# Routing steps of the expert passes in other slots, and the residual sum on GpSimd

## What is computed

```python
x = x + 0.5 * _L0_ffn_ref(_layernorm(x, axis=-1), ...)   # ffn0a
x = x + _L0_attn_ref(_layernorm(x, axis=-1), ...)
x = x + 0.5 * _L0_ffn_ref(_layernorm(x, axis=-1), ...)   # ffn0b
x = x + 0.5 * _L1_ffn_ref(_layernorm(x, axis=-1), ...)   # ffn1a
x = x + _L1_attn_ref(_layernorm(x, axis=-1), ...)
x = x + 0.5 * _L1_ffn_ref(_layernorm(x, axis=-1), ...)   # ffn1b
```

## Time and profile before

| | |
|---|---|
| median of three runs | 2052.0 us |
| profiled execution, its span | 2051.49 us, 2049.7 us |
| PE busy | 1723.2 us (84%) |
| VectorE, ScalarE, GpSimd busy | 1351.5, 1004.0, 736.8 us (66%, 49%, 36%) |
| granted PE clock, mean | 0.924 |

### The profile page before, as it was taken

How to read it: one execution, slowest core, us unless ns; L and a number is a source line. 1 busy time by engine, 2 the same in 40 slices (tenths; PEclk the granted TensorE clock), 3 DMA queues, 4 the chain that set the end, 5 groups by cost and what they waited for, 6 DMA issues and landing times. The chain is left out here.

```text
span 2049.7 us, 26334 instructions
## 1 busy us (share of the span) xinstructions
PE 1723.2 (84%) x8440; PEld 1206.2 (59%) x8440; DVE 1351.5 (66%) x4086; ACT 1004.0 (49%) x1687; POOL 736.8 (36%) x693
## 2 busy tenths in 40 slices
PE   3888869899899899968888699989967775989998
PEld 2666645545555555436666477767755664767776
DVE  4676658778778778536656466666667765666665
ACT  3555415555555565644554355455532223555554
POOL 3444411311312211114544355555520102555555
PEclk9999959999999999979888899999988897999999
DMA  4222211111110110003232211211100001121111
GB/s 130 84 78 69 64 28 30 18 24 28 18 34 18 21 31 18 10 25 103 78 104 74 95 42 42 75 50 42 42 1 0 0 0 42 51 84 47 47 52 52
DMA packets 58086, 94.98 MB, mean 46 GB/s; under 512 B 9297, under 2 KB 16850, under 8 KB 57954
## 3 DMA queue, kind: packets, MB, share of 16 engines
q1 hardware_dynamic: 55842, 91.08, 15.9%
q10 hardware_dynamic: 2112, 2.30, 0.4%
HBM read 76.76 MB, written 2.88 MB: 39 GB/s over the span
## 5 line engine op out<-in xcount | busy, mean ns | idle before, releaser
L909 ACT ACTIVATE att_probs<-banks 128x1024 f32<-128x1024 f32 (+3 forms) x384 | 306.1, 812 | 194.1 <-PE banks L820 192.0
L401 ACT ACTIVATE banks<-banks 128x512 f32<-128x512 f32 x384 | 223.3, 582 | 246.3 <-PE banks L319 239.9
L1034 DVE CUSTOM_DVE_ANT_0 banks<-banks,att_mask 128x128 f32<-128x128 f32 (+3 forms) x512 | 234.4, 525 | 70.6 <-PE banks L801 70.1
L801 PE MATMUL banks<-arena 128*128 128x512 f32 (+3 forms) x768 | 249.1, 406 | 27.9 <-DMA arena<-att_parts 15.3
L949 POOL TENSOR_SCALAR_AFFINE_SELECT att_probs<-att_probs 128x512 f32<-128x512 f32 x128 | 81.6, 637 | 419.7 <-ACT att_probs L909 419.7
L801 PEld LDWEIGHTS banks<-arena 128*128 128x128 f32 x768 | 132.7, 197 | 150.5 <-issue 90.8
L438 POOL TENSOR_TENSOR ffn1a_hid_l<-ffn1a_hid,ffn1a_hid_h 128x512 fp32r<-128x512 f32 x128 | 165.6, 1294 | 153.0 <-ACT ffn1a_hid_h L406 153.0
L438 POOL TENSOR_TENSOR ffn1b_hid_l<-ffn1b_hid,ffn1b_hid_h 128x512 fp32r<-128x512 f32 x128 | 165.3, 1292 | 152.1 <-ACT ffn1b_hid_h L406 152.1
L820 PE MATMUL banks<-arena 128*128 128x512 f32 (+3 forms) x768 | 204.4, 351 | 0.5 <-ACT att_probs L909 0.4
L1036 DVE TENSOR_REDUCE att_mx<-banks 128x1 f32<-128x512 f32 x256 | 162.2, 684 | 32.0 <-PE banks L801 31.8
L839 PE MATMUL banks<-att_probs,att_v_aug 128*32 128x512 f32 (+3 forms) x1536 | 166.4, 505 | 0.6 <-POOL att_probs L949 0.5
(11 more groups left out here) (390 smaller groups left out, 3890.8 us busy)
## 6 DMA issues: line engine op xcount, KB each, us to landing
ffn0a_share<-weight_rows SPq DMA_DIRECT2D x128, 128.0 KB, 3.0
ffn0b_share<-weight_rows SPq DMA_DIRECT2D x128, 128.0 KB, 3.0
ffn1a_share<-weight_rows SPq DMA_DIRECT2D x64, 256.0 KB, 4.3
ffn1b_share<-weight_rows SPq DMA_DIRECT2D x64, 256.0 KB, 4.5
arena<-att_parts SPq DMA_DIRECT2D x16, 384.0 KB
arena<-att_parts SPq DMA_DIRECT2D x128, 48.0 KB
w_raw<-in_ffn_w_dram SPq DMA_DIRECT2D x12, 256.0 KB, 3.2
out_dram<-x SPq DMA_DIRECT2D x8, 256.0 KB, 2.3
```

Of the source, the lines that this page charges most:

```text
L401: act.activation(gate if c < NSCALED else sil[:], gate, ACT.Silu).then_inc(silu_done, 1)
L801: mm = pe.matmul(bank[:, at:at + width], q_st[:, n % 3, t * P:(t + 1) * P], k_pad[:, n % 2, j, c * G:c * G + width], start=True, stop=True ...
L909: act.activation(probs[:, unit % NPROB, 2 * pair:2 * pair + 2, 0:c], score_ps[:, pair, :, 0:c], ACT.Exp, scale=SCALE).then_inc(exped, 1)
L1034: ins = dve.tensor_tensor_reduce(now, now, mask[:, G - width:G], 1.0, -3e38, ALU.add, ALU.max, best)
```

## The change

The table of slots is another one, and `norm` is cut in two steps of two tiles. In ffn0, `turn`, `xh` and `xl` become early steps: they are made for group h + 2 in the last slot, h's rows having been read. The routing is cut into r1 to r5 with the same instructions. The pieces go from slots 1 and NC // 2 to (3, 6) and (5, 10). The turned output is no longer read by VectorE: ScalarE copies it, halved, to SBUF (`take`), and GpSimd adds it to x (`add`). PE's waits on `misc` now ask for that copy (`y_read`).

```diff
--- before.py
+++ after.py
@@ -181,12 +181,14 @@
     ROUTE = 12 if first else 8
 
     if first:
-        slot = dict(stats=7, aggr=7, rstd=8, norm=8, turn=0, xh=0, xl=0, logit=2, lout=2, lturn=3,
-                    r1=3, r2=4, r3=5, r4=5, cturn=6, yout=2, yturn=4, y=4)
+        slot = dict(stats=0, aggr=1, rstd=1, norm=3, norm2=4, turn=8, xh=8, xl=8, logit=1, lout=1, lturn=2, r1=2, r2=2,
+                    r3=3, r4=4, r5=5, cturn=7, yout=2, yturn=5, y=6)
+        early = ("stats", "aggr", "rstd", "norm", "norm2", "turn", "xh", "xl")
     else:
-        slot = dict(stats=13, aggr=13, rstd=14, norm=14, turn=1, xh=1, xl=1, logit=3, lout=3, lturn=5,
-                    r1=5, r2=7, r3=9, r4=10, cturn=11, yout=2, yturn=7, y=8)
-    early = ("stats", "aggr", "rstd", "norm")
+        slot = dict(stats=11, aggr=12, rstd=12, norm=14, norm2=15, turn=1, xh=1, xl=1, logit=3, lout=3, lturn=4, r1=4,
+                    r2=5, r3=7, r4=8, r5=8, cturn=10, yout=2, yturn=6, y=7)
+        early = ("stats", "aggr", "rstd", "norm", "norm2")
+    PIECES = (3, 6) if first else (5, 10)
 
     def rows(g):
         return slice((g - g0) * G, (g - g0 + 1) * G)
@@ -206,8 +208,8 @@
                 f(g)
 
     def piece_at(g, c):
-        n = 2 * (g - g0 - 1) + (0 if c == 1 else 1)
-        return n if ahead is not None and g > g0 and c in (1, NC // 2) and n < ahead.count else None
+        n = 2 * (g - g0 - 1) + (0 if c == PIECES[0] else 1)
+        return n if ahead is not None and g > g0 and c in PIECES and n < ahead.count else None
 
     with ExitStack() as ctx:
         def sem(name):
...
@@ -242,7 +245,7 @@
         comb_turned, comb_t = sem("comb_turned"), sem("comb_t")
         rows_out = [sem(f"rows_out{q}") for q in range(2)]
         share_in = [sem(f"share_in{e}") for e in range(SLOTS)]
-        y_out, y_turned, y_added = sem("y_out"), sem("y_turned"), sem("y_added")
+        y_out, y_turned, y_read, y_added = sem("y_out"), sem("y_turned"), sem("y_read"), sem("y_added")
         gate_done, up_done, silu_done, scaled, hidden = (sem(s) for s in
             ("gate_done", "up_done", "silu_done", "scaled", "hidden"))
         high_cut, low_cut, down_done = sem("high_cut"), sem("low_cut"), sem("down_done")
@@ -307,6 +310,7 @@
 
             def cturn(g):
                 pe.wait_ge(route, (g + 1) * ROUTE)
+                at_least(pe, y_read, g - 1)
                 for t in range(TG):
                     mm = pe.transpose(misc[0:NE, t * P:(t + 1) * P], comb[:, t, :], k.ident)
                 mm.then_inc(comb_turned, 1)
@@ -343,7 +347,7 @@
                 elif g + 1 < end:
                     pe.wait_ge(comb_t, g + 2)
                 else:
-                    pe.wait_ge(y_added, g)
+                    pe.wait_ge(y_read, g)
                 for t in range(TG):
                     mm = pe.transpose(misc[:, t * P:(t + 1) * P], y_t[:, t * P:(t + 1) * P], k.ident)
                 mm.then_inc(y_turned, 1)
@@ -367,7 +371,12 @@
         def _(act):
             def norm(g):
                 act.wait_ge(rstd_done, 2 * g + 2)
-                for t in range(TG):
+                for t in range(TG // 2):
+                    act.activation(xn[:, t, :], k.x[:, tile_of(g, t)], ACT.Identity, bias=nshift[:, t:t + 1],
+                                   scale=rstd[:, t:t + 1])
+
+            def norm2(g):
+                for t in range(TG // 2, TG):
                     ins = act.activation(xn[:, t, :], k.x[:, tile_of(g, t)], ACT.Identity, bias=nshift[:, t:t + 1],
                                          scale=rstd[:, t:t + 1])
                 ins.then_inc(norm_done, 1)
@@ -410,19 +419,27 @@
                 at_least(act, y_turned, g)
                 act.activation(y_t[:], y_ps, ACT.Copy).then_inc(y_out, 1)
 
+            def take(g):
+                act.wait_ge(y_turned, g + 1)
+                at_least(act, y_added, g)
+                act.activation(y_tok[:], misc, ACT.Copy, scale=0.5).then_inc(y_read, 1)
+
             for h in range(g0 - 2, end):
                 for c in range(NC):
                     if h >= g0:
                         if slot["yout"] == c and h > g0:
                             yout(h - 1)
+                        if slot["y"] == c and h > g0:
+                            take(h - 1)
                         silu(h, c)
                         if h * NC + c > g0 * NC:
                             high(h * NC + c - 1)
                         if piece_at(h, c) is not None:
                             ahead.high(act, piece_at(h, c))
-                    chain(h, c, (("norm", norm), ("xh", xh), ("lout", lout), ("r1", r1), ("r2", r2), ("cturn", cturn)))
+                    chain(h, c, (("norm", norm), ("norm2", norm2), ("xh", xh), ("lout", lout), ("r1", r1), ("r2", r2), ("cturn", cturn)))
             high(end * NC - 1)
             yout(end - 1)
+            take(end - 1)
 
         @block.gpsimd
         def _(pool):
@@ -437,6 +454,10 @@
                 pool.wait_ge(high_cut, num + 1)
                 pool.tensor_tensor(hid_l[:, num % NH, :], hid[:, num % NH, :], hid_h[:, num % NH, :].bitcast(F32),
                                    ALU.subtract).then_inc(low_cut, 1)
+
+            def add(g):
+                pool.wait_ge(y_read, g + 1)
+                pool.tensor_tensor(k.x[:, rows(g)], k.x[:, rows(g)], y_tok[:], ALU.add).then_inc(y_added, 1)
 
             if ahead is not None:
                 ahead.clear(pool)
@@ -447,8 +468,11 @@
                             low(h * NC + c - 1)
                         if piece_at(h, c) is not None:
                             ahead.low(pool, piece_at(h, c))
+                        if slot["y"] == c and h > g0:
+                            add(h - 1)
                     chain(h, c, (("rstd", invert),))
             low(end * NC - 1)
+            add(end - 1)
 
         @block.vector
         def _(dve):
...
@@ -526,24 +559,15 @@
                     step(top(ext, top_sb), g)
                     step(dve.memset(top_sb[:, :, 4:8], PAD), g)
                 else:
-                    step(dve.memset(top_sb[:, :, 2:8], PAD), g)
-                pause(dve, k)
-                for t in range(TG):
-                    ins = dve.match_replace(mark[:, t, :], top_sb[:, t, :], ext[:, t, :], TAKEN)
-                step(ins, g)
-                if not first:
                     dve.wait_ge(tanh_done, g + 1)
                     step(dve.tensor_scalar(sig[:], th[:], 0.5, 0.5, ALU.mult, ALU.add), g)
 
-            def r4(g):
+            def r5(g):
+                if first:
+                    step(taken(ext, mark), g)
                 at_least(dve, comb_turned, g)
                 step(dve.scalar_tensor_tensor(comb[:], mark[:, :, 0:NE], TAKEN, sig[:], ALU.is_equal, ALU.mult), g)
                 assert count[0] == ROUTE, count[0]
-
-            def add(g):
-                dve.wait_ge(y_turned, g + 1)
-                dve.scalar_tensor_tensor(k.x[:, rows(g)], misc, 0.5, k.x[:, rows(g)], ALU.mult, ALU.add)\
-                   .then_inc(y_added, 1)
 
             def scale(g, c):
                 num, n = g * NC + c, g * NSCALED + c
@@ -568,14 +592,11 @@
             for h in range(g0 - 2, end):
                 for c in range(NC):
                     if h >= g0:
-                        if slot["y"] == c and h > g0:
-                            add(h - 1)
                         if c < NSCALED:
                             scale(h, c)
                         hide(h, c)
                     chain(h, c, (("stats", stats), ("aggr", aggr), ("xl", xl), ("r1", r1), ("r2", r2), ("r3", r3),
-                                 ("r4", r4)))
-            add(end - 1)
+                                 ("r4", r4), ("r5", r5)))
 
 
 def parcel(arena):
```

More of the change, by code:

```diff
@@ L232, in phase_moe @@
         hid_h, hid_l, y_t = sb("hid_h", [P, NH, G], F32R), sb("hid_l", [P, NH, G], F32R), sb("y_t", [P, G])
+        y_tok = sb("y_tok", [P, G])
         gate_ps, up_ps, y_ps, misc = k.banks[:, 0:3, :], k.banks[:, 3:6, :], k.banks[:, 6, :], k.banks[:, 7, :]
@@ L503, in r1, with taken @@
                     step(top(ext, top_sb), g)
+            def taken(rest, dst):
+                pause(dve, k)
+                for t in range(TG):
+                    ins = dve.match_replace(dst[:, t, :], top_sb[:, t, :], rest[:, t, :], TAKEN)
+                return ins
             def r2(g):
@@ L508, in r2 @@
                     step(dve.memset(top_sb[:, :, 2:8], PAD), g)
-                    pause(dve, k)
-                    for t in range(TG):
-                        ins = dve.match_replace(gmark[:, t, :], top_sb[:, t, :], gext[:, t, :], TAKEN)
-                    step(ins, g)
-                    step(dve.tensor_scalar(pen[:].rearrange("p (e t) -> p e t", t=TG),
-                                           gmark[:, :, 0:5].rearrange("p t e -> p e t"), TAKEN, OUT, ALU.not_equal,
-                                           ALU.mult), g)
                 else:
@@ L521, in r3, with r4 @@
             def r3(g):
```

(9 more changed lines are left out.)

## The result

Four runs of the changed kernel took 1934.5 to 1943.96, median 1936.8 us; four of the kernel before beside them had median 2063.2. The ratio is 0.9396, 95% interval [0.9315, 0.9478]: **faster by 6%**. The profiled execution took 1934.5 against 2051.49, 117.0 less where 84.8 was forecast; 1936.8 lies in the range given, 1.8 above its lower bound. The kernel before took 2030 to 2077 in all its runs, at a mean granted clock of 0.936 down to 0.908, so the clock of one stage in its trace belongs to that execution.

A forecast was written before the change was run, and what follows sets the result against it. PE bounds the expert passes, with holes in it. Gains of 20.9, 30.3, 21.2 and 16.8 over six groups per pass, minus 4.4 at the ends, make 84.8: 2051.5 to 1966.7, 1967 against the median, range 1935 to 1995.

The forecast's parts named there:

- the 2.96, 2.12 and 1.92: PE holes forecast to go: 2.96 in ffn1 at the normalizations, in ffn0 2.12 before turning rows, 1.92 before turning weights.
- The base of 37.1 in ffn1: ffn1's group period without its hole, before new delays are added: 40.23 - 2.96 - 0.16 = 37.1 us.
- that of 22.0 in ffn0: ffn0's group period without its three holes, before new delays are added: 27.24 down to 22.0 us.
- The inverse: ffn1, slot 12: GpSimd waits about 0.5 for VectorE, spends 1.3, and PE comes 1.0 late per group.
- The sum: Residual sum on GpSimd, 1.27 in a slot with 0.8 free: 0.5 on PE per group, bounds 0 and 1.3.
- The late broadcast: ffn0, weights turned in slot 7: VectorE waits 1.5 to 2.0 for their broadcast, 1.4 on PE per group.
- The 1.0 for the pieces: ffn0b: a weight piece of 1.30 shares slot 6 with the sum and slot 3 with norm, 1.0 more per group.
- The ends: Pass ends: later last sum costs 1.3 per pass, ffn1's last two groups 0.9; 4.4 lost in all.
- Everything new is covered: Rival, chance 0.12: PE's extra work hides all new delays; periods 22.1, 22.6, 37.2, 37.2, total 1925.
- The broadcast becomes the bound: Rival for ffn0, chance 0.18: hole at slots 2 and 3 reaches 2, the clock falls, adding 1.4; total 1994.
- The port: Rival, chance 0.04: added GpSimd work holds VectorE's routing steps, two per ffn0 group, one per ffn1 group; total 2010.
- the slower rival: Rival, chance 0.02: GpSimd's sum and inverse each idle PE over 2 per group, the clock falling after each; total 2093.

The follow-up runs named there:

- inverse3: The changed kernel with ffn1's statistics moved to slot 2 and aggregation and inverse to slot 3: 1931.1 us.
- cturn6: The changed kernel with the turning of ffn0's routing weights back in slot 6 instead of 7: 1923.7 us.
- sum8: The changed kernel with ffn1's residual sum in slot 8 instead of 7: 1940.6 us.
- sum_only: The kernel before with only the residual sum moved, ScalarE copying the turned output and GpSimd adding it: 2029.2 us, ratio 0.989.
- best: The changed kernel with the edits of cturn6 and inverse3 and the residual sum back on VectorE in its new slots: 1911.4 us.
- both: The changed kernel with the edits of cturn6 and inverse3, the sum staying on GpSimd: 1916.6 us.
- late_sum: The kernel before with ffn0's residual sum, still on VectorE, in slot 5 instead of 4: 2020.3 us, ratio 0.988.

## Why the prediction was right

**How near it was.** The range held by 1.8, and the gain was 117.0 in the trace for 84.8. The 32 too few are all on one side: 5.0 in ffn0a, 8.8 in ffn0b, 11.2 in the two of ffn1, 7.1 outside the periods. In ffn1 the measured 37.7 and 37.6 lie below even the 37.8 that the range allowed. So what follows is a right account of the holes with prices set too high. (The bounds of the groups add up to 1934 and 1990, not 1935 and 1995.)

**What bounds it, and the holes.** Right: the 2.96, 2.12 and 1.92 went with the steps named, the clock came up, and the holes behind the inverse and the broadcast stand where they were put. The one forecast two slots after the sum in ffn1 did not come. The base of 37.1 in ffn1 is 37.0 (`inverse3`), that of 22.0 in ffn0 is 21.9 (`cturn6`).

**The inverse, forecast 1.0, measured 0.59.** GpSimd waited 0.19, not 0.5, for VectorE, and its two instructions took 1.24. The next subtraction came 2.73 after the last, 0.6 beyond a slot.

**The sum, forecast 0.5 per group, measured 0 in ffn1.** This term was wrong, by 6 over the twelve periods of ffn1; in ffn0a too nothing of it shows (21.9 in `cturn6`, where 22.0 + 0.1 + 0.5 would be due). A slot was taken as 2.1; the one with the sum lasts 2.5, with or without the sum. In a plainer slot it costs 0.3 (`sum8`). ScalarE's copy was free in the changed kernel, as forecast: it starts at 1717.93 and the silu behind it is not late. It is not free in every slot: in `sum_only` it stood right behind the tanh, for which ScalarE had waited 1.65, the silu came late, and PE had a hole of 0.58 per group.

**The late broadcast, forecast 1.4, measured 1.28 in ffn0a**, with VectorE's wait 1.82 in the group shown and 1.8 to 2.7 over the six, forecast 1.5 to 2.0. In ffn0b it brought 0.58. The 1.0 for the pieces is right with the sum on GpSimd (22.9 in ffn0b against 21.9 in ffn0a in `cturn6`, with a hole of 1.05 behind the slot where piece and sum meet). With the sum on VectorE (`best`) both passes take 22.5 and that hole is gone, so the price is that of the two together. Added to the broadcast's it was too much, since the waits cover each other: 23.5, not 25.0. Those 8.8 are the largest miss of any one pass.

**The ends, forecast -4.4, measured +2.8 in all.** The cost of the later last sum is real: from the last turned logits of ffn1b to the end are 69.75 in `both` and 68.08 in `best`, 1.7 where 1.3 was forecast. What made up for it was not tested. The stretch with the first attention alone varies by 7 and more between traces, so 2.8 is no firm number.

**The rivals.** "Everything new is covered" gave 1925, 12 too fast: broadcast and inverse were not covered. "The broadcast becomes the bound" had the right mechanism, but its holes, 0.48 and 0.39 in the group shown and 1.35 at most, stayed below 2, and the clock stayed up. Its condition, that the clock falls from a hole of 2 on, holds only in some groups: the last three periods of ffn0a before have 2.11 to 2.15 at a clock of 1.00. The port did hold VectorE, 1.23 for an instruction that took 0.23 in `cturn6`, in the rows shown above; no loss beyond the two holes showed. Inside the six periods GpSimd's remainder never came more than 1.35 late for PE (in ffn0a, behind a broadcast 2.71 late; 1.15 in ffn1a, 1.08 in ffn0b), short of the 2 of the slower rival. The sum's move cost 5.5 (1936.8 against 1931.3), and 5.2 between `both` and `best`. The rule of the Trainium skill (GPSIMD Engine Reference, Engine selection), to keep such work on VectorE, is right in sign by these totals, though not in ffn0a alone (130.97 with the sum on GpSimd, 135.23 without); its 19 was too much, since most of the doubled time lies beside other work.

## What to carry to other kernels

Before moving work to another engine, move it by one slot: here the wait for an operand made in the same slot cost more than the engine's time (one number, 1.2%, against 5.5 us lost by the other engine). Price an addition by the length of the slot it falls in, not by the mean slot, and do not add the prices of two delays that stand close together. When a step is placed later, look for what reads its product through the slowest path (here DRAM), and place that step as early as its input is ready.

## What the runs showed of the hardware

The granted clock did not follow the holes alone. In ffn0b of the kernel before, holes of 0.75, 1.92 and 1.96 in each period of 30.7 went with 0.83. In ffn0a of the same trace, holes of 0.75, 1.91 and 2.15 went with 1.00 in three periods of 27.2. First one period of each, then the three holes of that ffn0a period, all from the kernel before:

```profile
1044.36:1075.06 30.70, 26.07 (x101) 19.76 (x100) 18.26 (x67) 15.33 (x29) 15.21 (x13) 0.83 0.28 87
185.03:212.26 27.23, 22.07 (x101) 16.79 (x100) 19.27 (x67) 14.26 (x27) 12.77 (x11) 1.00 0.27 79
192.33 0.50 PE L331 MATMUL banks<-ffn0a_hid_h,wdh 128*128 128x512 f32 x1 [0.75 <-POOL ffn0a_hid_l L438]
195.22 0.60 PE L311 MATMUL banks<-pack,ffn0a_comb 128*16 128x128 f32 x4 [1.91 <-DVE ffn0a_comb L540]
204.28 0.66 PE L292 MATMUL banks<-pack,ffn0a_xn 128*128 128x128 f32 x4 [2.15 <-ACT ffn0a_xn L371]
```

(That ffn0a period has one more hole, of 0.35.) In `late_sum`, with 1.46 to 1.63 and 2.10 to 2.15 in each period of ffn0b, three of 25.4 to 26.0 went at 1.00 and three of 27.0 to 27.1 at 0.94. So nearly the same holes go with either clock. What decides was not isolated, and a gain that comes with the clock (18.4 of the 21.8 in ffn0b there) is not shown to belong to the hole that was closed.
